# A two-convolution graph network on one core: the products of a finished tile are spread evenly over the visits of the next one

## The chip, the cores and the metric

The kernel runs on 1 core of one Trainium2 chip. The metric is the device time of one launch in microseconds (us), lower is better. The engines are named as in the profile: PE is TensorE's matmul stream and PEld its weight loads, DVE is VectorE, ACT is ScalarE, POOL is GpSimd, SP is SyncE. SPq and POOLq are the DMA issues of SP and POOL.

## The reference

There are 3,125 nodes of 1,024 features and 50,000 edges (`src` to `dst`, sorted by `dst`). A graph attention layer comes first, then the part that the change is in: two plain aggregates (mean over the neighbours), each followed by two products with 1,024 x 1,024 weights.

```python
def _sage_layer(h, edge_src, edge_dst, deg_inv, W_self, W_neigh, b):
    msg = h[edge_src]
    agg = jax.ops.segment_sum(msg, edge_dst, num_segments=h.shape[0])
    mean = agg * deg_inv[:, None]
    return h @ W_self + mean @ W_neigh + b
...
h = jax.nn.relu(_sage_layer(x, edge_src, edge_dst, deg_inv, W_self0, W_neigh0, b0))
out = _sage_layer(h, edge_src, edge_dst, deg_inv, W_self1, W_neigh1, b1)
...
h = jnp.maximum(_layernorm(x, axis=-1), 0.0)
x = x + _L1_gnn_ref(h, src, dst, L1_gnn_W_self0, L1_gnn_W_neigh0, L1_gnn_b0, L1_gnn_W_self1, L1_gnn_W_neigh1, L1_gnn_b1)
```

## The kernel before, in words

The program is a row of stages: tables of the edges, the attention layer's first product, its edge scores, its weighted sums (`weighted_sums`, gagg in the profile, a stage of gathers and short matmuls), `gat_finish`, then `first_layer` (agg0) and `last_layer` (agg1). Both of the last two have the same frame, and only they are changed.

**Numbers are kept in two halves.** A value is a pair of 16-bit floats, high and low, so a row is 2 x 1,024 values of 2 bytes (4 KB). A product with a weight that is also split takes three matmuls: high by high, high by low, low by high.

**Tiles and visits.** The nodes are cut into 25 tiles of 125 rows (`NT`, `TN`). The sum over the edges is made in 440 visits (`VISITS`), 17 or 18 for each tile. `place_of` lists them as pairs (i, n): tile i, and n, the number of the visit in the tile. A visit is:

- POOL gathers 128 rows of 4 KB by an indirect DMA into one of 7 buffers (`gather_visits`, L1885). It waits on `mm_done` of the visit 7 earlier.
- DVE makes the one-hot matrix `hot` 4 visits ahead (L1977, L2210).
- PE multiplies the gathered rows by it: `sum_window`, L1624, 16 matmuls of 64 columns into one of 3 PSUM buffers. It waits for `arrived` (the gather), `hot_ready`, and `added` of the visit 3 earlier.
- DVE adds the PSUM buffer to the sums in SBUF (L2016, L2240).

**A finished tile.** After the last visit of tile j, the sums of its rows are a factor of a product. ACT makes the high half (L2049, L2280), DVE the low half (`low`, L1983, L2216), and PE makes 48 products of 512 columns (`multiply`, L2095, L2318), in 12 pieces of 4. The pieces are put between the windows of the next tile, one in each of the visits n = `MULTIPLY_AT` to `MULTIPLY_AT` + 11. DVE reads the result out of PSUM (`read`, L1990, or the last operation of the last layer, L2250).

**The self part.** A tile's own rows are transposed by PE (`turn`, 16 transposes, L783), moved to SBUF by ACT (`move`, L2039, L2270) and multiplied by half of W_self1: 24 products of 512 columns (`multiply_self`, L2081, L2301). The first layer makes columns 0 to 511 of the last layer's self part and stores them (`part_rows`); the last layer makes columns 512 to 1,023. DVE reads them out (`read_part` L2001, `add_self` L2226). In the first layer the rows that are turned are the tile's output: DVE's `read`, ACT's relu and cast (L2056, L2061), DVE's `out_low` (L1994), `turn`.

**The order of the work** is written by hand. Each engine has its own loop over `place_of`, and the constants `LO_AT`, `MULTIPLY_AT`, `SELF_AT`, `TURN_AT` and so on say in which visit n a step is put, behind the window (PE) or the add (DVE) of that visit. Every engine works its list strictly in order, so a step that waits holds back the adds or windows behind it.

**SP's list in the last layer**, for each tile i: wait for `turned`, load the own rows of tile i + 1 (L2167); wait for `out_ready`, store the output of tile i - 1 (L2189); wait until it is stored; load x and the stored self part of tile i into the same buffers (`load_more`, L2172 and L2173). `add_self` waits for these loads, since its first operation adds them (L2223). Each transfer is two DMAs, of 112 and of 13 rows (`CUTS`).

Of the kernel before, what the change touches and what calls it, by code (L numbers as in the profile page):

```python
# [10 lines left out]
def bass_gat_sage_sage(nc, x_in, src_in, dst_in, w_gat, att_src, att_dst, gat_bias,  # L11
# [22 lines left out]
    NT = N // TN  # L34
# [112 lines left out]
    with top:  # L147
# [1742 lines left out]
        def first_layer(tag, flat, sums, mem):  # L1890

            with ExitStack() as ctx:
# [3 lines left out]
                AHEAD = 4  # L1896
                LO_AT, MULTIPLY_AT, READ_AT, OUT_AT = 0, 2, 14, 16
                PIECES = 12
                TURN_AT, SELF_AT, PART_AT = 1, 3, 15
                carve = carver(mem)  # L1900
# [67 lines left out]
                def _(v):  # L1968
# [57 lines left out]
                    v.wait_ge(added, VISITS)  # L2026
                    low(NT - 1)
                    read_part(NT - 2)
                    read(NT - 1)
# [4 lines left out]
                def _(a):  # L2034
# [9 lines left out]
                    for j in range(NT):  # L2044
                        tile = tile_reg_at(mybir.EngineType.Activation, j)
                        a.wait_ge(added, ended[j])
                        if j >= 1:
                            a.wait_ge(prod_done, j)
                        a.activation(as_turned(a_t, 0), by_feature(sums, tile), ACT.Copy, scale=sum_up[:, 0:1]).then_inc(hi_done, 1)  # L2049
                        if j >= 1:  # L2050
                            move(j - 1)
                        a.wait_ge(lo_done, j + 1)
                        a.activation(sums[:, ds(tile, 1), 0:D], ones[:, 0:1].to_broadcast([P, D]).rearrange("p (a d) -> p a d", a=1),
                                     ACT.Copy, scale=0.0).then_inc(zeroed, 1)
                        a.wait_ge(read_out, j + 1)
# [9 lines left out]
                def _(t):  # L2065
# [6 lines left out]
                    def multiply_self(j, piece):  # L2072
                        todo = half_products(half_ps, h_t, w_half)
                        per = len(todo) // PIECES
# [5 lines left out]
                        for o, l, r, start, stop in todo[piece * per:(piece + 1) * per]:  # L2080
                            last = t.matmul(o, l, r, start=start, stop=stop)  # L2081
                        if piece == PIECES - 1:
                            last.then_inc(self_done, 1)
# [15 lines left out]
                    for u, (i, n) in enumerate(place_of):  # L2099
# [12 lines left out]
                    for piece in range(PIECES):  # L2112
# [4 lines left out]
                    for piece in range(PIECES):  # L2117
                        multiply_self(NT - 1, piece)

        def last_layer(tag, flat, sums, mem):  # L2120

            with ExitStack() as ctx:
# [77 lines left out]
                def _(v):  # L2200
# [17 lines left out]

                    def add_self(j):
# [3 lines left out]
                        v.tensor_tensor(rows[:, :], rows[:, :], more[0:TN, :], ALU.add).then_inc(mixed, 1)  # L2223
                        v.wait_ge(mixed, j + 1)
                        v.wait_ge(self_done, j + 1)
# [7 lines left out]
                    for u, (i, n) in enumerate(place_of):  # L2233
# [8 lines left out]
                        if n == LO_AT and i >= 1:  # L2242
                            low(i - 1)
                        if n == ADD_AT and i >= 1:
                            add_self(i - 1)
# [5 lines left out]
                    v.wait_ge(added, VISITS)  # L2251
                    low(NT - 1)
                    add_self(NT - 1)
                    tile = tile_reg_at(mybir.EngineType.DVE, NT - 1)
                    v.wait_ge(self_read, NT)
# [29 lines left out]
                def _(t):  # L2285
# [6 lines left out]
                    def multiply_self(j, piece):  # L2292
                        todo = half_products(half_ps, h_t, w_half)
                        per = len(todo) // SELF_PIECES
# [5 lines left out]
                        for o, l, r, start, stop in todo[piece * per:(piece + 1) * per]:  # L2300
                            last = t.matmul(o, l, r, start=start, stop=stop)  # L2301
                        if piece == SELF_PIECES - 1:
                            last.then_inc(self_done, 1)
# [18 lines left out]
                    for u, (i, n) in enumerate(place_of):  # L2322
                        if n == 0:
                            turn(i)
# [63 lines left out]
```

## Time and profile before

| What | Value |
|---|---|
| Median of 3 runs | 3403.28 us (3386.56 to 3422.01) |
| Profiled execution: device time, span | 3406.57 us, 3404.8 us |
| PE busy | 2755.0 us (81%), 30361 matmuls |
| DVE busy | 2281.9 us (67%) |
| POOL busy | 1586.1 us (47%) |
| ACT busy | 1217.1 us (36%) |
| Moved by DMA | 923.25 MB, mean 271 GB/s |
| Granted TensorE clock | mean 0.911 |

The first layer lies between about 1610 and 2423 us of the span, the last layer from there to the end. Together they are more than half of the time. PEclk is the share of full speed that TensorE's clock had; it has two levels, 0.5 and 1.0. The DMA share is the mean busy time of the core's 16 DMA engines; over short stretches it can read a little above 1.

### The profile page before, as it was taken

The numbers are of one execution on the slowest core, as the hardware profiler recorded it, in microseconds if no ns is written. First come the engines' busy times: TensorE is split into PE (matmuls) and PEld (weight loads), VectorE is DVE, ScalarE is ACT, GpSimd is POOL, SyncE is SP. The second block draws the span as 40 slices with busy tenths as digits, with TensorE's granted clock in tenths as the row PEclk, the third lists the DMA queues.
The fourth block names the chain that finished last, engine by engine and source line by source line (L and its number), as shares of the span: only waits on it lengthen the run. The fifth ranks groups of instructions, "written<-read, shape, count | busy, mean of one in ns | idle before, by whom it ended". The sixth has DMA issues, their size and how long they took to land. (4 is left out here: it accounts for less than half of the span.)

```text
span 3404.8 us, 85744 instructions
## 1 busy us (share of the span) xinstructions
PE 2755.0 (81%) x30361; PEld 1840.4 (54%) x30361; DVE 2281.9 (67%) x4260; ACT 1217.1 (36%) x2842; POOL 1586.1 (47%) x1534
## 2 busy tenths in 40 slices
PE   5477898599999986997788888888567777777777
PEld 5244555388888863443555555555344444444444
DVE  7786778687888897885666666666245455555554
ACT  5464553698888863443122211221101000010010
POOL 2002232377777752222565655665244444454452
PEclk9878999799999998999798999999788888998888
DMA  2796995599999967775999988988588888898886
GB/s 77 244 294 211 323 325 175 170 340 348 354 348 352 349 213 242 224 217 187 355 317 303 317 303 307 311 305 277 212 257 270 258 269 246 264 286 256 262 284 190
DMA packets 282455, 923.25 MB, mean 271 GB/s; under 512 B 50690, under 2 KB 55790, under 8 KB 282030
## 3 DMA queue, kind: packets, MB, share of 16 engines
q0 software_dynamic: 209952, 697.51, 59.9%
q1 hardware_dynamic: 72078, 220.27, 21.0%
q8 instruction: 244, 4.00, 0.5%
q14 instruction: 181, 1.48, 0.1%
HBM read 857.98 MB, written 124.14 MB: 288 GB/s over the span
## 5 line engine op out<-in xcount | busy, mean ns | idle before, releaser
L1885 POOL DMA_INDIRECT agg_got<-h_rows,all_win_idx x756 | 780.2, 1032 | 775.3 <-PE agg_sum_ps L1624 583.2
L1614 PE MATMUL gagg_sum_ps<-gagg_got,gagg_hot_hi 128*128 128x256 f16 x3320 | 574.2, 273 | 63.9 <-DVE sums_acc L1560 27.1
L1624 PEld LDWEIGHTS agg_sum_ps<-all_mem,agg_got 128*128 128x128 f16 x12096 | 484.7, 103 | 240.1 <-issue 81.3
L1624 PE MATMUL agg_sum_ps<-all_mem,agg_got 128*128 128x64 f16 x12096 | 511.8, 200 | 80.8 <-DMA agg_got<-h_rows,all_win_idx 40.3
L1515 POOL DMA_INDIRECT gagg_got<-xs_rows,all_mem x415 | 465.0, 1120 | 167.8 <-issue 89.3
L1580 ACT ACTIVATE gagg_hot_hi<-gagg_hot,all_mem 128x128 f16<-128x128 f16 x1660 | 506.9, 387 | 84.1 <-DVE gagg_hot L1533 80.6
L2240 DVE TENSOR_TENSOR sums_acc<-agg_sum_ps,sums_acc 128x512 f32 x440 | 304.1, 691 | 287.7 <-PE agg_sum_ps L1624 283.2
L2016 DVE TENSOR_TENSOR sums_acc<-agg_sum_ps,sums_acc 128x512 f32 x440 | 303.7, 690 | 236.6 <-PE agg_sum_ps L1624 232.5
L1614 PE MATMUL gagg_sum_ps<-gagg_got,gagg_hot_lo 128*128 128x256 f16 x1660 | 453.7, 273 | 0.0
L2318 PE MATMUL agg_out_ps<-agg_w,all_mem 128*128 128x512 f16 x1152 | 341.6, 425 | 65.8 <-DVE all_mem L2216 65.8
L1614 PEld LDWEIGHTS gagg_sum_ps<-gagg_got,gagg_hot_hi 128*128 128x128 f16 x3320 | 285.7, 97 | 116.3 <-DVE sums_acc L1560 38.9
L2280 ACT ACTIVATE all_mem<-sums_acc,all_sum_up 128x1024 f16 x25 | 28.7, 1148 | 861.5 <-DVE sums_acc L2240 793.2
L2095 PE MATMUL agg_out_ps<-agg_w,all_mem 128*128 128x512 f16 x1200 | 318.9, 391 | 9.1 <-DVE all_mem L1983 8.8
L2301 PE MATMUL agg_half_ps<-agg_w_half,all_mem 128*128 128x512 f16 x600 | 179.7, 412 | 114.2 <-DVE all_mem L2226 110.4
L1538 DVE TENSOR_TENSOR gagg_hot_lo<-gagg_hot,all_mem 128x512 f16<-128x512 f16 x415 | 268.9, 687 | 4.0 <-DVE gagg_hot L1533 2.8
L1425 PE MATMUL edg_out_ps<-gatw_w,edg_a_t 128*128 128x512 f16 x1008 | 240.8, 383 | 17.7 <-ACT edg_rows L1233 17.6
L2056 ACT ACTIVATE all_mem<-all_mem,all_h_up 125x1024 f32<-125x1024 f32 x25 | 28.7, 1149 | 555.7 <-DVE all_mem L1990 555.7
L2318 PEld LDWEIGHTS agg_out_ps<-agg_w,all_mem 128*128 128x128 f16 x1152 | 101.7, 106 | 155.7 <-issue 102.1
L2081 PE MATMUL agg_half_ps<-agg_w_half,all_mem 128*128 128x512 f16 x600 | 179.4, 388 | 4.4 <-issue 4.4
L1885 POOL DMA_INDIRECT all_mem<-h_rows,all_win_idx x124 | 126.6, 1021 | 110.1 <-PE agg_sum_ps L1624 93.8
L1872 PE MATMUL fin_out_ps<-fin_w,all_mem 128*128 128x512 f16 x800 | 176.7, 379 | 0.0
L1614 PEld LDWEIGHTS gagg_sum_ps<-gagg_got,gagg_hot_lo 128*128 128x128 f16 x1660 | 162.2, 98 | 20.2
(404 smaller groups left out, 4084.9 us busy)
## 6 DMA issues: line engine op xcount, KB each, us to landing
gatw_piece<-slot_rows POOLq DMA_DIRECT2D x52, 512.0 KB
split_w<-edg_w_out SPq DMA_DIRECT2D x32, 512.0 KB, 8.8
x_rows<-fin_val POOLq DMA_DIRECT2D x25, 500.0 KB
h_rows<-fin_h POOLq DMA_DIRECT2D x25, 500.0 KB, 8.2
agg_got<-h_rows,all_win_idx POOLq DMA_INDIRECT x756
norm_x_sb<-in_x_dram SPq DMA_DIRECT2D x25, 448.0 KB
fin_x_sb<-in_x_dram SPq DMA_DIRECT2D x25, 448.0 KB
all_mem<-xp_rows SPq DMA_DIRECT2D x25, 448.0 KB
```

Source lines behind the costliest of these rows:

```text
L1425: last = t.matmul(o, l, r, start=start, stop=stop)
L1515: g.indirect_dma_start(out=got[:, u % R, :], out_offset=None, in_=rows_in[:, :], in_offset=bass.IndirectOffsetOnAxis(ap=set_idx[:, col:col ...
L1538: v.tensor_tensor(hot_lo[:, u % HOTS, :, :], hot[:, u % HOTS:u % HOTS + 1, :].to_broadcast([P, H, P]), weight_e[:, ds(begins[g] + j, 1), 1 ...
L1580: last = a.activation(hot_hi[:, u % HOTS, h, :], hot[:, u % HOTS, :], ACT.Copy, scale=high_e[:, ds(begins[g] + j, 1), h])
L1614: last = t.matmul(sum_ps[g % 2][:, h * C:(h + 1) * C], hot_k[:, u % HOTS, h, :], got[:, u % R, part * D + h * C:part * D + (h + 1) * C], s ...
L1624: last = t.matmul(sum_ps[:, k * WIN:(k + 1) * WIN], got_u[:, part * D + k * P:part * D + (k + 1) * P], hot_u, start=(part == 0), stop=(par ...
L1885: g.indirect_dma_start(out=got[u % slots], out_offset=None, in_=rows_in[:, :], in_offset=bass.IndirectOffsetOnAxis(ap=win_idx[:, u:u + 1], ...
L2016: v.tensor_tensor(window_of(flat, at), sum_ps[u % SUMS][:, :].rearrange("p (k d) -> p k d", k=KT), window_of(flat, at), ALU.add).then_inc( ...
L2095: last = t.matmul(o, l, r, start=start, stop=stop)
L2240: v.tensor_tensor(window_of(flat, at), sum_ps[u % SUMS][:, :].rearrange("p (k d) -> p k d", k=KT), window_of(flat, at), ALU.add).then_inc( ...
L2301: last = t.matmul(o, l, r, start=start, stop=stop)
L2318: last = t.matmul(o, l, r, start=start, stop=stop)
```

## The change

The constants of both layers are set anew, and three steps move in the text of the program.

- **PE.** In the first layer, the 48 products move from n = 2 to 13 to n = 3 to 14; the self part's 24 products, before 2 in each of n = 3 to 14 beside the 4 of the other product, go to five visits of their own: 5, 5, 5, 5 and 4 at n = 15, 16, 0, 1, 2. `turn` goes from n = 1 to n = 3. In the last layer the products move in the same way from n = 2 to 13 to n = 3 to 14, the self part from 3 in each of n = 7 to 14 to the same five visits, and `turn` from n = 0 to n = 13.
- **DVE.** `low` goes from n = 0 to 1 in both. In the first layer `read` goes from 14 to 15, `out_low` from 16 to 0 of the tile after, `read_part` from 15 to 4 of the tile after. In the last layer `add_self` is cut in two: `mix` (the add of what was loaded) at n = 12 and the read-out of the self part at n = 13, where both stood at n = 5; the last operation of a tile goes from 14 to 15.
- **ACT.** In the first layer, `move` comes behind the clearing of the sums and no more ahead of it.

Nothing is added and nothing taken away: the number of matmuls, of DVE and ACT operations and of DMAs is the same.

```diff
-                LO_AT, MULTIPLY_AT, READ_AT, OUT_AT = 0, 2, 14, 16
+                OUT_AT, LO_AT, MULTIPLY_AT, READ_AT = 0, 1, 3, 15
                 PIECES = 12
-                TURN_AT, SELF_AT, PART_AT = 1, 3, 15
+                TURN_AT, PART_AT = 3, 4
+                SELF_AT = (15, 16, 0, 1, 2)
...
+                        if n == OUT_AT and i >= 2:
+                            out_low(i - 2)
                         if n == LO_AT and i >= 1:
                             low(i - 1)
+                        if n == PART_AT and i >= 3:
+                            read_part(i - 3)
                         if n == READ_AT and i >= 1:
                             read(i - 1)
-                        if n == PART_AT and i >= 2:
-                            read_part(i - 2)
-                        if n == OUT_AT and i >= 1:
-                            out_low(i - 1)
...
-                        if SELF_AT <= n < SELF_AT + PIECES and i >= 2:
-                            multiply_self(i - 2, n - SELF_AT)
+                        if n in SELF_AT:
+                            piece = SELF_AT.index(n)
+                            j = i - 2 if piece < 2 else i - 3
+                            if j >= 0:
+                                multiply_self(j, piece)
...
-                LO_AT, MULTIPLY_AT, ADD_AT, DONE_AT = 0, 2, 5, 14
+                LO_AT, MULTIPLY_AT, MIX_AT, ADD_AT, TURN_AT, DONE_AT = 1, 3, 12, 13, 13, 15
                 PIECES = 12
-                SELF_AT, SELF_PIECES = 7, 8
+                SELF_AT = (15, 16, 0, 1, 2)
...
-                        if SELF_AT <= n < SELF_AT + SELF_PIECES:
-                            multiply_self(i, n - SELF_AT)
+                        if n in SELF_AT:
+                            piece = SELF_AT.index(n)
+                            j = i if piece < 2 else i - 1
+                            if j >= 0:
+                                multiply_self(j, piece)
+                    for piece in range(2, len(SELF_AT)):
+                        multiply_self(NT - 1, piece)
```

PE in the last layer, at the turn from one tile to the next, before. agg_sum_ps is written by the windows, agg_half_ps by the self products, agg_turn_ps by `turn`, agg_out_ps by the 48 products.

```order
L2301 MATMUL agg_half_ps<-agg_w_half,all_mem 128x512 x3
L1624 MATMUL agg_sum_ps<-all_mem,agg_got 128x64 x48
L783 MATMUL agg_turn_ps<-all_ident,all_mem 128x128 x16
L1624 MATMUL agg_sum_ps<-all_mem,agg_got 128x64 x16
L1624 MATMUL agg_sum_ps<-all_mem 128x64 x16
L1624 MATMUL agg_sum_ps<-all_mem,agg_got 128x64 x16
L2318 MATMUL agg_out_ps<-agg_w,all_mem 128x512 x4
```

The same place after the change (L2314 is the self product, L2331 the other):

```order
L2314 MATMUL agg_half_ps<-agg_w_half,all_mem 128x512 x5
L1624 MATMUL agg_sum_ps<-all_mem,agg_got 128x64 x16
L2314 MATMUL agg_half_ps<-agg_w_half,all_mem 128x512 x5
L1624 MATMUL agg_sum_ps<-all_mem,agg_got 128x64 x16
L2314 MATMUL agg_half_ps<-agg_w_half,all_mem 128x512 x4
L1624 MATMUL agg_sum_ps<-all_mem,agg_got 128x64 x16
L2331 MATMUL agg_out_ps<-agg_w,all_mem 128x512 x4
```

Six windows in a row with only `turn` between them have become windows with 4 or 5 products behind each.

DVE in the last layer, where the loaded rows and the self part are taken in, before (n = 5). The ISA and TENSOR_LOAD rows read a register; L2223 is the add of what SP loaded, L2226 reads the self part.

```order
L2240 ISA
L2240 TENSOR_TENSOR sums_acc<-agg_sum_ps,sums_acc 128x8x64
L2223 TENSOR_TENSOR all_mem<-all_mem 125x1024
L2226 SCALAR_TENSOR_TENSOR all_mem<-agg_half_ps,agg_post_self,all_mem 125x512
L196 TENSOR_LOAD all_win_at
```

After (n = 12 and n = 13; L2231 is the add, L2236 the read-out):

```order
L2250 TENSOR_TENSOR sums_acc<-agg_sum_ps,sums_acc 128x8x64
L2231 TENSOR_TENSOR all_mem<-all_mem 125x1024
L196 TENSOR_LOAD all_win_at
L196 ISA x2
L2218 TENSOR_SCALAR all_mem<-all_iota_tn,all_win_rel 128x64
L2250 ISA
L2250 TENSOR_TENSOR sums_acc<-agg_sum_ps,sums_acc 128x8x64
L2236 SCALAR_TENSOR_TENSOR all_mem<-agg_half_ps,agg_post_self,all_mem 125x512
```

The pair has moved seven visits towards the end of the tile, and a visit's work now stands between its two operations.

## Rows read from the trace of the kernel before

**Rows 1.** Busy time by stretch: gather stage gagg, first layer, last layer
```profile
core 0: us, PE busy (x) PEld busy (x) DVE busy (x) ACT busy (x) POOL busy (x), PEclk, DMA share, GB/s
700.00:1100.00 400.00, 387.26 (x3928) 339.25 (x3926) 323.78 (x633) 345.98 (x1193) 315.00 (x280) 1.00 0.96 351
1736.87:2382.66 645.79, 559.79 (x7753) 367.96 (x7751) 418.69 (x820) 128.33 (x106) 382.36 (x363) 0.93 0.89 306
2516.66:3384.26 867.60, 663.45 (x8456) 408.08 (x8456) 460.90 (x898) 67.01 (x47) 402.01 (x398) 0.88 0.86 263
```

**Rows 2.** ACT's high half, once a tile, 22 of the first layer: start, duration, [idle before]
```profile
1736.87 1.15 ACT L2049 ACTIVATE all_mem<-sums_acc,all_sum_up 128x1024 f16 x1 [2.14 <-DVE sums_acc L2016]
...
2382.66 1.15 ACT L2049 ACTIVATE all_mem<-sums_acc,all_sum_up 128x1024 f16 x1 [1.98 <-DVE sums_acc L2016]
```

**Rows 3.** The same, 24 of the last layer, first and last
```profile
2516.66 1.15 ACT L2280 ACTIVATE all_mem<-sums_acc,all_sum_up 128x1024 f16 x1 [28.27 <-DVE sums_acc L2240]
...
3384.26 1.15 ACT L2280 ACTIVATE all_mem<-sums_acc,all_sum_up 128x1024 f16 x1 [32.58 <-DVE sums_acc L2240]
```

**Rows 4.** Who waited for whom, 1737 to 2383 us: total, times, longest
```profile
PE agg_turn_ps L783 <- DVE all_mem L1994: 60.7, 21, 4.0
```

**Rows 5.** Who waited for whom, 2517 to 3384 us
```profile
DVE all_mem L2223 <- DMA all_mem<-part_rows: 124.0, 23, 10.1
...
PE agg_half_ps L2301 <- DVE all_mem L2226: 110.4, 23, 9.6
...
PE agg_out_ps L2318 <- DVE all_mem L2216: 65.0, 23, 3.7
```

**Rows 6.** Timeline of PE at full clock: windows, and turn
```profile
2060.14 0.63 PE L1624 MATMUL agg_sum_ps<-all_mem,agg_got 128*128 128x64 f16 x16
2060.60 1.03 PE L2095 MATMUL agg_out_ps<-agg_w,all_mem 128*128 128x512 f16 x4
...
2061.90 0.63 PE L1624 MATMUL agg_sum_ps<-all_mem,agg_got 128*128 128x64 f16 x16
...
2899.96 0.63 PE L1624 MATMUL agg_sum_ps<-all_mem,agg_got 128*128 128x64 f16 x16
2900.43 1.06 PE L783 MATMUL agg_turn_ps<-all_ident,all_mem 128*128 128x128 f16 x16
2901.70 0.63 PE L1624 MATMUL agg_sum_ps<-all_mem,agg_got 128*128 128x64 f16 x16 [0.21 <-DVE sums_acc L2240]
```

**Rows 7.** Timeline of POOL, gathers with free buffers
```profile
2071.66 0.99 POOL L1885 DMA_INDIRECT agg_got<-h_rows,all_win_idx  x1 [0.30 <-PE agg_sum_ps L1624]
2072.96 0.99 POOL L1885 DMA_INDIRECT agg_got<-h_rows,all_win_idx  x1 [0.30 <-issue]
```

**Rows 8.** Timeline of one tile's output, store and loads, last layer
```profile
2899.51 1.28 DVE L2250 SCALAR_TENSOR_TENSOR all_mem<-agg_out_ps,agg_post,all_mem 125x1024 f32<-125x1024 f32 x1
...
2906.90 0.35 SPq L2172 DMA_DIRECT2D all_mem<-x_rows  x1
...
2920.22 1.22 DVE L2223 TENSOR_TENSOR all_mem<-all_mem 125x1024 f32<-125x1024 f32 x1 [6.43 <-DMA all_mem<-part_rows]
```

**Rows 9.** Timeline from a tile's last add to its first product
```profile
2903.51 0.69 DVE L2240 TENSOR_TENSOR sums_acc<-agg_sum_ps,sums_acc 128x512 f32 x1
...
2904.33 1.15 ACT L2280 ACTIVATE all_mem<-sums_acc,all_sum_up 128x1024 f16 x1 [36.88 <-DVE sums_acc L2240]
...
2907.17 1.02 PE L2318 MATMUL agg_out_ps<-agg_w,all_mem 128*128 128x512 f16 x4 [2.19 <-DVE all_mem L2216]
```

**Rows 10.** Busy time in stretches of 2 us (columns as in Rows 1)
```profile
2056.00:2058.00 2.00, 2.00 (x25) 1.17 (x24) 1.15 (x3) 0.00 (x0) 0.99 (x1) 1.00 1.03 419
...
2904.00:2906.00 2.00, 0.63 (x16) 0.54 (x16) 1.48 (x4) 1.67 (x2) 1.39 (x3) 1.00 0.92 271
2906.00:2908.00 2.00, 0.83 (x4) 0.42 (x5) 1.96 (x5) 1.25 (x1) 1.78 (x1) 1.00 0.93 322
2908.00:2910.00 2.00, 2.00 (x21) 1.14 (x20) 1.73 (x4) 0.00 (x0) 1.30 (x2) 0.58 0.89 287
```

More of the change, by code:

```diff
@@ L2017, in _ @@
                                         ALU.add).then_inc(added, 1)
+                        if n == OUT_AT and i >= 2:
+                            out_low(i - 2)
                         if n == LO_AT and i >= 1:
                             low(i - 1)
+                        if n == PART_AT and i >= 3:
+                            read_part(i - 3)
                         if n == READ_AT and i >= 1:
                             read(i - 1)
-                        if n == PART_AT and i >= 2:
-                            read_part(i - 2)
-                        if n == OUT_AT and i >= 1:
-                            out_low(i - 1)
                     v.wait_ge(added, VISITS)
+                    out_low(NT - 2)
                     low(NT - 1)
+                    read_part(NT - 3)
                     read_part(NT - 2)
@@ L2049, in _ @@
                         a.activation(as_turned(a_t, 0), by_feature(sums, tile), ACT.Copy, scale=sum_up[:, 0:1]).then_inc(hi_done, 1)
-                        if j >= 1:
-                            move(j - 1)
                         a.wait_ge(lo_done, j + 1)
@@ L2054, in _ @@
                                      ACT.Copy, scale=0.0).then_inc(zeroed, 1)
+                        if j >= 1:
+                            move(j - 1)
                         a.wait_ge(read_out, j + 1)
@@ L2073, in multiply_self @@
                         todo = half_products(half_ps, h_t, w_half)
-                        per = len(todo) // PIECES
+                        last_piece = len(SELF_AT) - 1
                         if piece == 0:
@@ L2079, in multiply_self @@
                                 t.wait_ge(part_ready, j)
-                        for o, l, r, start, stop in todo[piece * per:(piece + 1) * per]:
+                        for o, l, r, start, stop in todo[5 * piece:5 * (piece + 1)]:
                             last = t.matmul(o, l, r, start=start, stop=stop)
-                        if piece == PIECES - 1:
+                        if piece == last_piece:
                             last.then_inc(self_done, 1)
@@ L2108, in _ @@
                             multiply(i - 1, n - MULTIPLY_AT)
-                        if SELF_AT <= n < SELF_AT + PIECES and i >= 2:
-                            multiply_self(i - 2, n - SELF_AT)
+                        if n in SELF_AT:
[4 more added lines that the diff above has]
+                    for piece in range(2, len(SELF_AT)):
+                        multiply_self(NT - 3, piece)
                     turn(NT - 2)
-                    for piece in range(PIECES):
+                    for piece in range(len(SELF_AT)):
                         multiply_self(NT - 2, piece)
@@ L2116, in _ @@
                     turn(NT - 1)
-                    for piece in range(PIECES):
+                    for piece in range(len(SELF_AT)):
                         multiply_self(NT - 1, piece)
@@ L2217, in low, with mix @@
                                                ALU.mult, ALU.subtract).then_inc(lo_done, 1)
-                    def add_self(j):
+                    def mix(j):
                         v.wait_ge(x1_loaded, CUT * (j + 1))
@@ L2223, in add_self @@
                         v.tensor_tensor(rows[:, :], rows[:, :], more[0:TN, :], ALU.add).then_inc(mixed, 1)
+                    def add_self(j):
                         v.wait_ge(mixed, j + 1)
@@ L2243, in _ @@
                             low(i - 1)
+                        if n == MIX_AT and i >= 1:
+                            mix(i - 1)
                         if n == ADD_AT and i >= 1:
@@ L2252, in _ @@
                     low(NT - 1)
+                    mix(NT - 1)
                     add_self(NT - 1)
@@ L2293, in multiply_self @@
                         todo = half_products(half_ps, h_t, w_half)
-                        per = len(todo) // SELF_PIECES
+                        last_piece = len(SELF_AT) - 1
                         if piece == 0:
@@ L2299, in multiply_self @@
                                 t.wait_ge(self_read, j)
-                        for o, l, r, start, stop in todo[piece * per:(piece + 1) * per]:
+                        for o, l, r, start, stop in todo[5 * piece:5 * (piece + 1)]:
                             last = t.matmul(o, l, r, start=start, stop=stop)
-                        if piece == SELF_PIECES - 1:
+                        if piece == last_piece:
                             last.then_inc(self_done, 1)
@@ L2322, in _ @@
                     for u, (i, n) in enumerate(place_of):
-                        if n == 0:
+                        if n == TURN_AT:
                             turn(i)
@@ L2331, in _ @@
                             multiply(i - 1, n - MULTIPLY_AT)
-                        if SELF_AT <= n < SELF_AT + SELF_PIECES:
-                            multiply_self(i, n - SELF_AT)
+                        if n in SELF_AT:
[3 more added lines that the diff above has]
+                                multiply_self(j, piece)
+                    for piece in range(2, len(SELF_AT)):
+                        multiply_self(NT - 1, piece)
                     ready(NT - 1)
```

## The prediction

> **What bounds the kernel now.** I read the profile's page first: PE is busy 81% of the span, more than any other, so it looks like the bound. The busy time by stretch corrects this [rows 1]. In the gather stage before the two layers PE is busy 387.26 of 400 us at clock 1.00, and the DMA engines, at share 0.96, move 351 GB/s. In the first layer PE is busy 87%, the DMA share is 0.89 and the rate 306 GB/s; in the last layer 76%, 0.86 and 263. Neither engine is full in either layer: they take turns.
>
> Next, the time of one tile, from the operation that ACT makes once a tile. First layer: (2382.66 - 1736.87) / 21 = 30.75 us [rows 2]. Last layer: (3384.26 - 2516.66) / 23 = 37.72 us [rows 3].
>
> Then the waits. In the first layer PE stands before `turn` 21 times, 60.7 us in all, so 2.9 us a tile, for DVE's `out_low` (L1994) [rows 4]. In the last layer DVE waits 124.0 us for the loads of x and the stored self part, 23 times, 5.4 us each; PE waits 110.4 us for the read-out behind that add, 4.8 us a tile, and 65.0 us, 2.8 a tile, for the low half [rows 5]. The 5.4 and the 4.8 are one stall seen from two engines.
>
> Last, the pace of single visits. A first-layer visit with window, 4 products and 2 self products takes 2061.90 - 2060.14 = 1.76 us, of which the window is 2060.60 - 2060.14 = 0.46, so a product is 1.30 / 6 = 0.217 us; `turn` costs PE 2901.70 - 2900.43 = 1.27 us [rows 6]. A visit with no product behind it is as fast as POOL issues gathers, 2072.96 - 2071.66 = 1.30 us [rows 7].
>
> **The floors of a tile.** 440 / 25 = 17.6 visits, 72 products, one `turn`.
>
> - PE at full clock: 17.6 x 0.46 + 72 x 0.217 + 1.27 = 8.1 + 15.6 + 1.3 = 25.0 us.
> - POOL: 17.6 x 1.30 = 22.9 us. DVE: 418.69 / 21 = 19.9 and 460.90 / 23 = 20.0 us [rows 1].
> - Bytes: 306 GB/s x 30.75 us = 9.41 MB, and 263 x 37.72 = 9.92 MB.
>
> So before, twelve visits of a first-layer tile are PE's (21.1 us, in which the gathers run only as fast as buffers come free) and the rest are POOL's and the waits'. If the same 72 products are 4 or 5 in each visit, a visit costs PE 0.46 + 4 x 0.217 = 1.33 or 0.46 + 5 x 0.217 = 1.55 us, near what POOL needs, and what binds next is the transfers. The bound of their time comes from two sides:
>
> - Below: the rate of the gather stage, 351 GB/s. 9.41 / 0.351 = 26.8 us and 9.92 / 0.351 = 28.3 us. That stage has no loads and stores of SP in between.
> - Above: packets go on taking as long as in the layer itself. 306 / 0.89 x 0.96 = 330 GB/s gives 28.5 us; 263 / 0.86 x 0.96 = 294 GB/s gives 33.8 us.
>
> I take 27.6 us for the first layer, the middle: its rate in short stretches reaches 419 GB/s [rows 10]. For the last I take 31.7 us, above its middle of 31.1, since SP's transfers are more there and each visit can now wait for its gather.
>
> **The waits, step by step.** A shorter tile needs each wait gone and none new.
>
> - First layer, `turn`. `out_low` is at n = 0 and `turn` at n = 3; `read` at n = 15 starts relu and cast on ACT, about 2.3 us, beside two visits. PE then has n = 0, 1, 2, 1.55 + 1.55 + 1.33 = 4.4 us, against DVE's 1.2. The 2.9 us go.
> - Low half, both layers. Last add to first product is 2907.17 - 2903.51 = 3.66 us [rows 9]. `low` and the first product keep their distance of two visits, but the windows ahead of it now carry products: from the end of the last window PE has 4.4 + 0.46 = 4.9 us of work (6.2 with `turn`). `low` stands behind the adds of n = 0 and 1, the second of which can begin at 2.0 us, so it ends near 4.2. The 2.8 us go, with 0.7 us to spare; if they did not, they would cost at most 2.8 again.
> - Last layer, loads. The chain is the last operation of a tile (L2250), store, wait for it, loads, add: 2920.22 - 2899.51 = 20.7 us to the add's start, of which 13.3 are from the first load's issue [rows 8]. It had from n = 14 to n = 5, 8.6 visits; it gets n = 15 to n = 12, 14.6 visits, 14.6 x 31.7 / 17.6 = 26.3 us. `load_row`, released by `turn` at n = 13 instead of n = 0, now goes into SP's queue ahead of the store: 0.5 MB, some 2 us. Spare: 3.6 us. The 5.4 us go. If the loads are late, DVE stands at n = 12 with its adds behind it, and PE stops within three windows, since there are three PSUM buffers.
> - Last layer, own rows. `turn` at n = 13, then ACT's move of some 2 us, against PE's 0.46 + 0.87 + 1.33 + 0.46 = 3.1 us to the first self product at n = 15: hidden.
> - ACT's `move` behind the clearing of the sums: ACT is busy 128.33 of 645.79 us; hidden by 12 visits.
>
> **The sum**, against the profiled execution's 3406.6 us (the three runs have the median 3403.3, 0.1% off). First layer: 22 tiles with all their products x (30.75 - 27.6 = 3.15) = 69 us. Last layer: 23 x (37.72 - 31.7 = 6.0) = 138 us. The start of the last layer is full of transfers of weights and stays, but its self products no more wait for their weights and the second tile has the stall too: 10 us. At the ends of both layers 14 self products come behind the last window, 3 us each, where PE waits for the low half anyway: 0. 3406.6 - 69 - 138 - 10 = 3190 us (3189.6).
>
> **Rivals.**
>
> 1. The transfers reach the gather stage's rate. 22 x 3.95 + 23 x 9.4 + 10 = 313 us: 3093. For it: the share there is 0.96 with PE just as busy. Against: SP's transfers. The Trainium skill (DMA: Bandwidth & Descriptors, Specifications) gives a limit of about 358 GB/s from HBM for one core. By that figure tiles would take 26.3 and 27.7 us, an estimate that makes the sum 3069. The stage's 351 agrees, the 419 GB/s of one stretch [rows 10] is above it.
> 2. Packets keep today's mean time, 28.5 and 33.8 us. 22 x 2.25 + 23 x 3.9 = 140 us: 3267.
> 3. The change does half of what it says: SP's chain is drawn out, since the DMA engines are now full all through the tile, and the last layer's stall only moves to n = 12. Then only the first layer gains: 3406.6 - 69 = 3338. It needs a chain of over 14.6 / 17.6 x 37.7 = 31 us instead of 20.7.
> 4. Slower: the clock. PE falls to the 0.5 level after 2 us stretches in which it was busy 0.63 and 0.83 us [rows 10]; each tile now has such drops, mean 0.93 and 0.88 [rows 1]. If PE, short of gathers, idles a little in every visit, the drops could come all through the tile. At a mean of 0.68 its 25.0 us become 36.8: 22 x (36.8 - 30.75) - 23 x (37.72 - 36.8) = 133 - 21 = +112 us, 3518. It begins to be slower where the mean falls under 25.0 / 34.3 = 0.73. Against: a PE that is slowed is busy again, and in the gather stage it stayed at 1.00 for 400 us. The Trainium skill (TensorE: Matmul & The Clock Gate, "A second HAM failure mode: psum-queue depth-cycling") tells of a kernel whose short idle times between groups of matmuls made the clock go up and down. By that rule this rival is the case; the trace shows drops only behind stretches with long idle time.
>
> **How the numbers follow.** Forecast 3190: 0.50. Rival 1: 0.16. Rival 2: 0.19. Rival 3: 0.08. Rival 4: 0.04. The rest, 0.03, is within 1%. A measurement of this kernel tells about 1% from no change, 34 us, so faster is under 3369: 0.50 + 0.16 + 0.19 + 0.08 = 0.93. I give 0.91, and 0.05 to same, for what I have not seen in the waits. The range goes from rival 1 to a little above rival 2: 3090 to 3290.
>
> **What would show it.** Right: the once-a-tile operation of ACT comes every 27 to 28 and 31 to 32 us; DMA share 0.94 or more and 320 to 345 GB/s in both layers; PE's waits for L1994, L2216 and L2226 near zero; its waits are now for gathers, and short. Wrong: DVE waits 2 us or more a tile at the add at n = 12 (rival 3); PEclk under 0.85 (rival 4); a share near 0.96 at 300 GB/s or less (rival 2).

## The result, and the profile after

The changed kernel takes 3112.18 us (median of 4 runs, 3109.58 to 3119.44), the one before 3398.49 us in the same runs: ratio 0.9153, 95% interval 0.9100 to 0.9207. The forecast was 3190 us in a range of 3090 to 3290. The direction came out as forecast, and the waits that the forecast named went; the size is 1.3 times as large, 286 us in place of 217.

The busy time by stretch of the changed kernel: the gather stage, then the first and the last layer (columns as in [rows 1], which these answer to).

```profile
700.00:1100.00 400.00, 390.45 (x3968) 342.67 (x3965) 328.04 (x638) 349.84 (x1207) 314.39 (x282) 1.00 0.97 354
1724.77:2295.96 571.19, 529.27 (x7756) 332.31 (x7755) 416.24 (x819) 127.58 (x106) 382.47 (x364) 1.00 0.96 346
2417.41:3090.16 672.75, 587.14 (x8492) 362.30 (x8491) 457.55 (x898) 69.58 (x46) 421.85 (x399) 1.00 1.01 341
```

The gather stage has not moved. The two layers do the same work in less time: the DMA share went from 0.89 to 0.96 and from 0.86 to 1.01, the clock from 0.93 and 0.88 to 1.00. The stretches run from one high half of ACT to another, so they give the time of a tile: 571.19 / 21 = 27.20 us (before 30.75 [rows 2]) and 672.75 / 23 = 29.25 us (before 37.72 [rows 3]).

Who waited for whom in the first layer of the changed kernel, against [rows 4]:

```profile
POOL agg_got L1885 <- issue: 86.5, 211, 3.2
PEld agg_sum_ps L1624 <- DMA agg_got<-h_rows,all_win_idx: 73.0, 93, 2.5
...
PE agg_sum_ps L1624 <- DMA agg_got<-h_rows,all_win_idx: 35.9, 50, 2.0
```

And in the last layer, against [rows 5]:

```profile
PE agg_sum_ps L1624 <- DMA agg_got<-h_rows,all_win_idx: 76.0, 82, 2.6
...
DVE all_mem L2231 <- DMA all_mem<-part_rows: 1.2, 1, 1.2
PE agg_out_ps L2331 <- DVE all_mem L2224: 0.7, 1, 0.7
```

All four waits that the prediction named are gone: 60.7 us before `turn` to nothing, 124.0 to 1.2, 110.4 to nothing, 65.0 to 0.7. What PE now waits for are gathers, many times and briefly.

The profile's chain of work that ended last, in shares of the span, names the same thing. Before, its largest piece was `all_mem<-part_rows`, the loads behind the stall:

```profile
DMA all_mem<-part_rows 6%; PE agg_out_ps L2318 4%; DMA out_dram<-all_mem 4%; PE agg_half_ps L2301 4%; PE agg_sum_ps L1624 3%; SPq L2172 1%; DVE all_mem L2250 1%; DVE all_mem L2223 1%; DMA all_mem<-h_rows 1%; DVE all_mem L2226 1%; SPq L788 0%; SPq L2173 0%; PE agg_out_ps L2338 0%; SPq L2189 0%; DVE sums_acc L2240 0%
```

After, it is the gathers:

```profile
DMA 14%; issue 5%; POOL 3%; PE 3%; DVE 0%; ACT 0%; POOLq 0%; DVEq 0%; ACTq 0%
DMA agg_got<-h_rows,all_win_idx 11%; POOL agg_got L1885 3%; DMA all_mem<-h_rows,all_win_idx 2%; PE agg_sum_ps L1624 1%; PE agg_half_ps L2314 1%; PE agg_out_ps L2331 0%; POOL all_mem L1885 0%; PE agg_out_ps L2356 0%; PE agg_turn_ps L783 0%; DVE all_mem L2224 0%; ACT all_mem L2293 0%; DVE all_mem L2209 0%; DVE agg_got L2239 0%; POOLq L1884 0%; DVE all_mem L2275 0%
```

Twelve kernels follow. Their tiles are measured in the same way, here from the second high half of each layer to the last. Each ratio is against runs of the kernel before on the same chip, whose median was 3389.76 to 3404.7 us. Each tile comes from one profiled execution. Kernels with the very same layer differ there by up to 0.3 us in the changed first layer (26.8 to 27.1), 0.2 in the changed last one (29.2 to 29.4) and 0.7 in the last one of before (37.0 and 37.7), so smaller differences show nothing. In short:

| Run | Time (us) | Ratio, 95% interval | Tile of first, last layer (us) |
|---|---|---|---|
| before | 3398.49 | 1 | 30.8, 37.7 |
| changed | 3112.18 | 0.9153 (0.9100 to 0.9207) | 27.1, 29.3 |
| e1 first layer only | 3307.08 | 0.9718 (0.9672 to 0.9765) | 26.9, 37.0 |
| e2 last layer only | 3199.95 | 0.9407 (0.9375 to 0.9439) | 30.9, 29.2 |
| e3 loads' add at n = 5 | 3263.76 | 0.9602 (0.9570 to 0.9634) | 26.9, 35.8 |
| e4 uneven, stall gone | 3278.14 | 0.9648 (0.9615 to 0.9681) | 30.5, 32.3 |
| e5 half the gathers, changed | 2950.09 | 0.8686 (0.8645 to 0.8726) | 24.8, 25.4 |
| e6 half the gathers, before | 3248.91 | 0.9565 (0.9518 to 0.9612) | 30.7, 32.3 |
| e7 1 of 24 self products | 3096.51 | 0.9117 (0.9064 to 0.9169) | 26.8, 29.6 |
| e8 before, PE kept busy | 3378.73 | 0.9953 (0.9924 to 0.9983) | 30.1, 37.6 |
| e9 uneven, DVE spread | 3200.78 | 0.9403 (0.9372 to 0.9433) | 30.7, 29.3 |
| e10 own rows behind loads | 3152.68 | 0.9267 (0.9241 to 0.9293) | 26.8, 31.1 |
| e11 `turn` at n = 1 | 3122.75 | 0.9174 (0.9149 to 0.9200) | 27.3, 29.4 |
| e12 own rows later | 3149.42 | 0.9276 (0.9246 to 0.9306) | 26.8, 31.2 |

### The profile page after: what moved, and what is told of

It reads as the page before. It is cut to its first block and busy times, and to the rows that moved or that the text cites. A ratio compares the mean times of both kernels' runs of the same rounds, so it can differ in the third digit from the quotient of the medians.

```text
span 3107.8 us, 85745 instructions
## 1 busy us (share of the span) xinstructions
PE 2645.8 (85%) x30361; PEld 1756.8 (57%) x30361; DVE 2278.2 (73%) x4260; ACT 1219.4 (39%) x2842; POOL 1598.8 (51%) x1534
## 5 line engine op out<-in xcount | busy, mean ns | idle before, releaser
L1885 POOL DMA_INDIRECT agg_got<-h_rows,all_win_idx x756 | 788.8, 1043 | 513.0 <-PE agg_sum_ps L1624 217.0
L1624 PEld LDWEIGHTS agg_sum_ps<-all_mem,agg_got 128*128 128x128 f16 x12096 | 447.6, 100 | 379.9 <-DMA agg_got<-h_rows,all_win_idx 277.1
L1624 PE MATMUL agg_sum_ps<-all_mem,agg_got 128*128 128x64 f16 x12096 | 489.4, 196 | 177.1 <-DMA agg_got<-h_rows,all_win_idx 176.3
L1614 PEld LDWEIGHTS gagg_sum_ps<-gagg_got,gagg_hot_hi 128*128 128x128 f16 x3320 | 286.1, 97 | 111.2 <-DVE sums_acc L1560 37.6
L2098 PE MATMUL agg_out_ps<-agg_w,all_mem 128*128 128x512 f16 x1200 | 309.0, 382 | 0.0
L2331 PE MATMUL agg_out_ps<-agg_w,all_mem 128*128 128x512 f16 x1152 | 297.9, 381 | 0.7 <-DVE all_mem L2224 0.7
L2283 ACT ACTIVATE all_mem<-agg_turn_ps 128x2048 f16<-128x2048 f16 x25 | 46.9, 1877 | 545.8 <-PE agg_turn_ps L783 545.8
L1533 DVE TENSOR_SCALAR gagg_hot<-all_iota_tn,all_mem 128x128 f16<-128x128 f32 x415 | 112.1, 292 | 85.5 <-PE gagg_sum_ps L1614 84.8
L1560 DVE TENSOR_TENSOR sums_acc<-gagg_sum_ps,sums_acc 125x1033 f32 x135 | 165.7, 1228 | 5.3 <-PE gagg_sum_ps L1614 2.3
L1885 POOL DMA_INDIRECT all_mem<-h_rows,all_win_idx x124 | 135.1, 1090 | 65.7 <-issue 36.9
L1425 PEld LDWEIGHTS edg_out_ps<-gatw_w,edg_a_t 128*128 128x128 f16 x1008 | 93.2, 99 | 114.6 <-issue 25.2
```

The source lines that it names most:

```text
L1614: last = t.matmul(sum_ps[g % 2][:, h * C:(h + 1) * C], hot_k[:, u % HOTS, h, :], got[:, u % R, part * D + h * C:part * D + (h + 1) * C], s ...
L1624: last = t.matmul(sum_ps[:, k * WIN:(k + 1) * WIN], got_u[:, part * D + k * P:part * D + (k + 1) * P], hot_u, start=(part == 0), stop=(par ...
L1885: g.indirect_dma_start(out=got[u % slots], out_offset=None, in_=rows_in[:, :], in_offset=bass.IndirectOffsetOnAxis(ap=win_idx[:, u:u + 1], ...
```

## The experiments

**Each layer alone (e1, e2).** The edit is the change, in one of the two functions only.

> The change in the first layer alone; the last layer is the one of before. The traces give the first layer's share as 84 us (24 tiles, 30.6 to 27.1 us each), so about 3315 us if the two layers' gains simply add. If the first layer's gain needs the last layer's (or a slower one follows from it), the two single runs don't add up to 286 us.

> The change in the last layer alone. By the traces 195 us in 23 tiles (37.7 to 29.25 us) and 17 us at its start and end: about 3188 us, tile 29.3 us.

Measured: 3307.08 us and 3199.95 us. The ratios take off 2.8% and 5.9%, together 8.7%, and the whole change 8.5%: the two gains add within their intervals. Two thirds are the last layer's.

**The stall back, the products even (e3).** In the last layer:

```diff
-                LO_AT, MULTIPLY_AT, MIX_AT, ADD_AT, TURN_AT, DONE_AT = 1, 3, 12, 13, 13, 15
+                LO_AT, MULTIPLY_AT, MIX_AT, ADD_AT, TURN_AT, DONE_AT = 1, 3, 5, 13, 13, 15
```

> The changed kernel, but in the last layer the add of the loaded rows stands at n = 5 again, with all else spread as it is. If the old stall was SP's chain of store, wait and loads (20.7 us, against 7.6 visits x 1.66 = 12.6 us), it comes back with 6 to 8 us: tile about 35 to 36 us, 3250 to 3270 us, DVE waits 100 us or more for the loads. If an even spread alone made the difference, the loads land in time and the kernel stays at 3112 us.

Measured: 3263.76 us, 35.8 us a tile. The waits of its last layer:

```profile
DVE all_mem L2231 <- DMA all_mem<-part_rows: 223.4, 23, 11.7
PEld agg_sum_ps L1624 <- issue: 203.7, 88, 10.3
PE agg_sum_ps L1624 <- DVE sums_acc L2250: 174.6, 23, 9.8
```

The loads are late by 9.7 us each time, and since DVE's adds queue behind the waiting one, PE stops three windows later for 7.6 us. So the stall was SP's chain of store, wait and loads, and what took it away is the place of one add, 7 visits later: 6.5 us a tile against the changed kernel. The stall is longer here than before (5.4 us [rows 5]). Two reasons lie in the lists, not tested apart: the last operation of a tile, which releases the store, stands at n = 15 and not 14, and the load of the own rows now goes ahead of the store.

**The stall gone, the products uneven (e4).** The later read-outs stay; the self products go back beside the others, one tile later:

```diff
-                SELF_AT = (15, 16, 0, 1, 2)
+                SELF_AT = tuple(range(3, 15))
...
-                        for o, l, r, start, stop in todo[5 * piece:5 * (piece + 1)]:
+                        for o, l, r, start, stop in todo[2 * piece:2 * (piece + 1)]:
```

(with `PART_AT` = 15 in the first layer, `ADD_AT` = 15 and `TURN_AT` = 1 in the last).

> The changed kernel with its later read-outs and loads, but the self part's 24 products again 2 in each of n = 3 to 14 beside the 4 of the other product (6 products in 12 visits, none in the others), one tile later, in both layers. Theory that the transfers set the pace and 7 buffers smooth the rest: first layer 28.5 us, last 30 us a tile, about 3160 us. Rival, that light visits cost what they did (POOL's pace there and the clock's drops behind them): first layer back at 30.7, last 31 or more, about 3230 us. Rival, that only the waits mattered: 3112 us.

Measured: 3278.14 us, worse than all three expected. The busy time of its two layers, and one wait of each:

```profile
1727.30:2372.98 645.68, 571.34 (x7748) 373.82 (x7746) 416.02 (x820) 129.79 (x107) 373.06 (x363) 0.93 0.89 306
2508.72:3250.85 742.13, 633.77 (x8470) 394.39 (x8471) 456.66 (x898) 69.59 (x47) 426.11 (x398) 0.92 0.95 308
...
PE agg_turn_ps L783 <- DVE all_mem L1995: 31.5, 21, 2.1
...
PE agg_out_ps L2331 <- DVE all_mem L2224: 56.5, 23, 3.6
```

The first of these lines is that of the kernel before, digit for digit in the clock, the share and the rate. So the first of the two rivals, that the light visits (those without products) cost what they did, is right for the first layer: without the even order nothing is gained there. The wait before `turn` is not gone here but halved, 1.5 us a tile in place of 2.9; e9 below takes it away wholly. My own theory, that 7 buffers smooth the rest, fell. In the last layer both count. With e3 they make a rough square: 37.7 us with neither, 35.8 with the even order only, 32.3 with only the stall gone, 29.25 with both. It is rough because e3's stall is longer than that of before, and because in e4 PE still waits 2.5 us a tile for the low half (2.8 before): that wait goes with the even order (1.2 us in all 23 tiles of e3).

**What in the uneven visits costs the time (e8, e9).** First the clock. e8 is the kernel before, with work of no use ahead of the windows where PE was idle:

```diff
+                        if i >= 1 and (n >= 15 or n <= 1):
+                            for _ in range(4):
+                                t.matmul(sum_ps[u % SUMS][:, :], w_half[:, 0, 0, 0:P], w_half[:, 0, 0, :], start=True, stop=True)
```

(from tile 3 on in the first layer).

> The kernel before with 4 products of no use put ahead of the windows of n = 15, 16, 17, 0 and 1 in both layers: more work for PE, in the visits where it was near idle and its clock fell behind them. If the clock's drops cost time by themselves, the first layer falls by 1 to 2 us a tile and the last by 1 to 3, in spite of more work: about 3320 us, PEclk over 0.95. If only the waits cost time, it stays at 3400 us or goes above.

Measured: 3378.73 us. The first layer:

```profile
1730.10:2360.77 630.67, 605.74 (x8137) 378.02 (x8135) 418.07 (x820) 128.23 (x105) 369.47 (x363) 1.00 0.90 313
```

The clock is at 1.00, and a tile takes 30.1 us, 0.7 less, with more work in it: 384 matmuls more in 21 tiles, at 0.217 us 4.0 us a tile. In the last layer the mean clock rose only to 0.92, with DVE still waiting for the loads 23 times, and the tile stayed within 0.1 us. The 0.7 us are a net figure, since the added work may cost time too: the drops cost at least that. They can't have cost more than about 2.2 us of the 30.75 (an estimate: all that a mean clock of 0.93 withholds, (1 - 0.93) x 30.75, as if every moment of it held up the tile). So of the first layer's 3.6 us, 1.4 or more have another cause than the clock. The whole kernel gained 0.5%, much less than the 3320 us expected.

Second, DVE. e9 has e4's first layer, with DVE's `out_low` and `read_part` taken out of the light visits' neighbourhood:

```diff
-                OUT_AT, LO_AT, MULTIPLY_AT, READ_AT = 0, 1, 3, 15
+                OUT_AT, LO_AT, MULTIPLY_AT, READ_AT = 4, 1, 3, 15
...
-                TURN_AT, PART_AT = 3, 15
+                TURN_AT, PART_AT = 7, 2
```

> The changed kernel with the uneven first layer of the fourth run (6 products in each of n = 3 to 14), but DVE's out_low at n = 4, turn at n = 7 and read_part at n = 2: two of DVE's per-tile operations leave the light visits' neighbourhood n = 15 to 0, and turn (1.3 us of PE) goes among the dense ones. The last layer is the changed one. In the fourth run the first layer took 30.7 us a tile, and in the light visits PE waited for DVE's adds. If DVE's crowding there sets them (5.6 light visits x 0.88 + 1.28 + 1.23 + 0.75 + 1.28 = 9.5 us, with 21.1 us of dense visits 30.6), the tile falls by about 1 us, to 29.7. If unevenness as such costs the 3.6 us (POOL's pace in the light visits and the clock), it stays at 30.7: 3112 + 24 x 3.6 = about 3200 us.

Measured: 3200.78 us, 30.7 us a tile: no gain. Its largest waits of PE in the first layer:

```profile
PE agg_out_ps L2099 <- DVE all_mem L1984: 39.6, 21, 2.6
PE agg_sum_ps L1624 <- DVE sums_acc L2017: 36.3, 36, 1.9
```

No wait before `turn` is left, so that wait by itself was worth nothing. The wait has another name each time, L1994 before, DVE's adds and `turn` in e4, the low half and the adds here, and the tile is 30.5 to 30.8 us in all three. Twelve visits at 1.76 us, 21.1 us, are PE's in all of them, so about 9.6 us go to the five or six light visits. What may bind there is the chain of the last add, ACT's high half, DVE's low half and the first product, 3.66 us [rows 9], which bare windows of 0.46 us don't cover; that is argued, not tested. POOL's pace of 1.30 us a visit, the other half of the rival, is not what PE waits for: its waits for `agg_got` are 4.3 us in all 640 us here. That one order's wait comes back as another's is shown; why the sum is so nearly the same in all three is not.

**Are the transfers the bound now? (e5, e6, e7)** Half of the gathers' bytes are left out (rows with a number of 1562 or more are not fetched), which leaves all other work as it is:

```diff
-            last_row = g.to_reg(N - 1)
+            last_row = g.to_reg(N // 2 - 1)
```

> The changed kernel, but rows with a number of 1562 or more are not gathered in the two layers (half of the gathers' bytes left out, same number of gathers and all the matmuls). If the transfers set the time, the tiles fall to PE's 25.0 us (27.1 and 29.25 now): 24 x 2.1 + 23 x 4.25 = about 150 us less, 2960 us, PE busy over 97%. If PE or the order sets it, it stays at 3112 us.

> The kernel before with the same half of the gathers' bytes left out. Theory: its first layer is set by PE in the dense visits, POOL in the light ones and the wait before turn, not by bytes: 30 to 30.7 us a tile. Its last layer waits for SP's chain, which runs faster through emptier DMA engines: 31 to 34 us. About 3250 to 3320 us in all. If bytes set both layers before as well, it falls as far as the changed kernel does, to 3250 us or less with the first layer under 28 us.

> The changed kernel with 1 of the 24 self products in each tile (23 left out, 5.0 us of PE work a tile). Transfer theory: the last layer's tile stays within 1 us of 29.25 and the first layer falls from 27.1 to 25 to 26 us (9.41 MB at 370 to 385 GB/s): about 3050 us. Rival, PE sets the pace: 5.0 us less in each of 47 tiles, about 2880 us.

The changed kernel with half the gathers:

```profile
1713.96:2234.98 521.02, 518.86 (x7756) 338.40 (x7755) 416.32 (x819) 127.46 (x107) 381.94 (x364) 1.00 0.74 217
2348.66:2932.15 583.49, 572.28 (x8492) 370.65 (x8491) 456.68 (x898) 69.59 (x47) 420.05 (x399) 1.00 0.83 233
```

PE is busy 99.6% and 98.1%, and a tile takes 24.8 and 25.4 us, where PE's own 25.0 us had been worked out. The kernel before with the same half:

```profile
1727.20:2371.80 644.60, 559.28 (x7756) 367.76 (x7754) 418.56 (x820) 128.26 (x105) 381.49 (x363) 0.93 0.62 175
2490.50:3232.34 741.84, 624.62 (x8456) 392.41 (x8456) 460.67 (x898) 67.00 (x46) 416.20 (x399) 0.93 0.68 183
```

Its first layer does not move, with the DMA engines busy 62%: the bytes left out were not on the path. Its last layer gains 5.5 us a tile; there the wait for the loads fell from 124.0 to 46.8 us, so the chain of the loads got shorter. The total alone, 3248.91 us, would have fitted the rival too (3250 us or less); the first layer decides, and it was to be under 28 us for that. And with 23 of the 24 self products left out of the changed kernel:

```profile
1723.05:2288.11 565.06, 465.26 (x7254) 310.86 (x7254) 413.93 (x819) 127.43 (x107) 378.07 (x363) 0.94 0.97 350
2402.99:3083.81 680.82, 528.10 (x7960) 348.55 (x7960) 456.89 (x898) 69.58 (x46) 418.01 (x399) 0.89 1.00 337
```

5.0 us of PE work less a tile give nothing beyond the spread of single executions in the first layer (26.8 us; other kernels with the changed first layer have 26.8 to 27.1) and nothing in the last. POOL has the same number of gathers to issue in e5, whose tiles are shorter, so it is not the bound either. So the transfers set the pace of both layers now, in the first even more so than I had expected (25 to 26 us; 9.41 MB at the rates named with it even make 24.4 to 25.4).

**Where SP's transfers stand (e10, e12).** The rate at which full DMA engines move bytes was the number that I had wrong. In the kernel before, SP sends its loads in one go from 2906.90 on [rows 8]: x, the stored self part and the own rows, 1.25 MB. In the changed one the own rows go apart. e10 puts them together again:

```diff
-                        if i + 1 < NT:
-                            sp.wait_ge(turned, i + 1)
-                            load_row(i + 1)
                         if i >= 1:
...
                             load_more(i)
+                        if i + 1 < NT:
+                            sp.wait_ge(turned, i + 1)
+                            load_row(i + 1)
```

> The changed kernel, but in the last layer SP issues the load of a tile's own rows right behind the loads of x and the stored self part, so 1.25 MB come in one row as in the kernel before, instead of 0.75 and 0.5 MB apart. Theory that bunched loads of SP beside full gather buffers lower the rate (before, 306 GB/s at full share; after, 338): the last layer's tile rises from 29.25 to 30.5 to 32 us, 3140 to 3175 us. Rival, that the rate depends on the mix of bytes alone: 3112 us.

Measured: 3152.68 us, 31.1 us a tile, the same bytes. Its last layer:

```profile
2418.09:3132.82 714.73, 596.45 (x8492) 373.21 (x8491) 456.32 (x898) 69.60 (x47) 426.79 (x399) 0.98 0.98 321
```

Stretches of 3 us of it, from SP's loads on (the first is issued at 2826.8, the own rows at 2831.6):

```profile
2826.00:2829.00 3.00, 3.00 (x42) 1.86 (x43) 2.54 (x7) 0.00 (x0) 2.29 (x3) 1.00 1.01 376
2829.00:2832.00 3.00, 3.00 (x43) 1.90 (x42) 2.17 (x5) 0.00 (x0) 2.23 (x3) 1.00 1.03 326
2832.00:2835.00 3.00, 1.83 (x29) 0.98 (x28) 1.40 (x4) 0.00 (x0) 1.98 (x2) 1.00 1.02 281
2835.00:2838.00 3.00, 1.49 (x26) 0.77 (x23) 0.91 (x2) 0.00 (x0) 0.99 (x1) 1.00 1.05 270
2838.00:2841.00 3.00, 1.31 (x20) 0.58 (x16) 0.92 (x2) 0.00 (x0) 0.99 (x1) 1.00 1.04 287
2841.00:2844.00 3.00, 2.85 (x41) 1.66 (x42) 1.50 (x3) 0.00 (x0) 0.99 (x1) 1.00 1.03 366
```

The engines are full in all six, and for 9 us they move 270 to 287 GB/s, against 366 and 376 at the two ends, while PE is busy half the time for want of gathers. In the changed kernel the dip behind the loads is shorter, and a second one comes where the own rows (issued at 2823.9) and the store (2828.5) now stand; PE is busy all through that one:

```profile
2809.00:2812.00 3.00, 3.00 (x47) 1.87 (x43) 1.91 (x5) 0.00 (x0) 2.32 (x3) 1.00 1.05 360
2812.00:2815.00 3.00, 2.58 (x40) 1.54 (x39) 1.75 (x4) 0.00 (x0) 2.23 (x3) 1.00 1.02 289
2815.00:2818.00 3.00, 1.51 (x23) 0.78 (x20) 0.91 (x2) 0.00 (x0) 0.99 (x1) 1.00 1.05 293
2818.00:2821.00 3.00, 2.69 (x42) 1.50 (x39) 1.57 (x3) 0.00 (x0) 1.33 (x2) 1.00 1.02 371
...
2824.00:2827.00 3.00, 3.00 (x45) 1.84 (x43) 2.51 (x6) 0.84 (x1) 2.09 (x3) 1.00 0.94 298
2827.00:2830.00 3.00, 3.00 (x43) 1.88 (x42) 2.96 (x6) 0.81 (x1) 1.90 (x3) 1.00 1.02 259
```

The slower rate is not all of e10's 1.8 us. Divided by the share, its last layer moves 321 / 0.98 = 328 GB/s at full share, the changed one 341 / 1.01 = 338: 3% for the rate, and another 3% for engines that are less full. With the latter goes a wait for the low half that is back:

```profile
PE agg_out_ps L2331 <- DVE all_mem L2224: 17.5, 21, 1.4
```

e12 was to make use of that. It is e10 with one more wait ahead of the own rows:

```diff
+                            sp.wait_ge(mm_done, ended[i] + 7)
```

> A try at a faster version: the changed kernel, but SP issues the load of a tile's own rows when the 8th visit or so of the tile has begun (it waits for mm_done), between the loads of x and the store, instead of right ahead of the store. Theory that SP's transfers cost less the further apart they come (the run before, with 1.25 MB in one row, rose to 31.1 us a tile, 319 GB/s): the tile falls from 29.25 to 28.5 to 29.0 us, 3095 to 3108 us. Rival, that the gap is wide enough already or that a late load of the rows makes turn wait at n = 13: 3112 us or more.

Measured: 3149.42 us, 37 us above the changed kernel. SP's issues in it show why:

```profile
2819.53 0.35 SPq L2180 DMA_DIRECT2D all_mem<-x_rows  x1
...
2824.21 0.87 SPq L2175 DMA_DIRECT2D all_mem<-h_rows  x2
```

Store and wait take so long that the loads of x start only 4.7 us ahead of the visit that I had picked, and the own rows are in the same bunch as in e10. The try tells nothing about a real gap. No run that does all the work was faster than the changed kernel.

**Only the wait before `turn` back (e11).** In the first layer:

```diff
-                OUT_AT, LO_AT, MULTIPLY_AT, READ_AT = 0, 1, 3, 15
+                OUT_AT, LO_AT, MULTIPLY_AT, READ_AT = 16, 1, 3, 15
...
-                TURN_AT, PART_AT = 3, 4
+                TURN_AT, PART_AT = 1, 4
```

(`out_low` again for the tile whose `read` was the visit before.)

> The changed kernel, but in the first layer out_low and turn are where they were (n = 16 of the same tile, n = 1), with the even products. PE waits 1 to 2 us a tile before turn again, by the lists. If the transfers set the tile's time there too, that wait is covered (PE's 25.0 + 1.5 is under 27.1): 27.1 to 27.5 us, 3112 to 3120 us. If each wait of PE is paid in full, the tile is 28.6 us or more: 3150 us.

Measured: 3122.75 us, 27.3 us a tile. PE waits for L1995 again:

```profile
PE agg_turn_ps L783 <- DVE all_mem L1995: 27.9, 20, 2.0
```

That is 1.4 us a tile, half of the 2.9 before, and the tile is 0.2 to 0.5 us above those of the other kernels with the changed first layer. The whole kernel is 10.6 us slower by the medians, 0.4 us for each of 24 tiles, but the two ratios' intervals overlap. So the wait is mostly covered. Gathers land during it: PE's own waits for `agg_got` fell from 35.9 us to 10.0.

## Why the prediction was right, and where its size was off

- **What bounds it before: right that no engine is full, wrong that PE and the DMA engines take turns in the first layer.** If they did, half the bytes would have shortened it; in e6 the tile stayed at 30.7 us. PE waited there for DVE and, in the kernel before, for practically no gather (0.2 us in 646). The prediction's other account of the same tile, twelve visits of PE's and the rest POOL's and the waits', is nearer, but without POOL, since a PE that followed POOL's pace would be waiting for gathers.
- **The waits: right that all go, wrong about one price.** The walk through the four chains held: three of them left nothing, the loads 1.2 us in 23 tiles. But the 2.9 us before `turn` were named among the causes of the first layer's time. e9 and e11 show that they have no such price: with them gone and the products uneven nothing is gained, with half of them back and the products even 0.2 to 0.5 us are lost. No term of the sum rested on it, since the tile was worked out from the transfers.
- **The floors: right.** 25.0 us for PE, measured as 24.8 and 25.4 in e5.
- **First layer, 22 x 3.15 = 69 us: 22 x 3.55 = 78 measured** (27.2 us in place of 27.6).
- **Last layer, 23 x 6.0 = 138 us: 23 x 8.47 = 195 measured.** This is the term that was mis-sized. The step was the choice of 31.7 us, "above its middle", between 28.3 and 33.8. The upper end took two things from the layer as it was: a share of 0.96 at most, which became 1.01, and packets as slow as then, 306 GB/s at full share, which became 341 / 1.01 = 338. The slowness belonged in part to the order being changed: e10, with SP's loads together again, takes 1.8 us a tile more for unchanged bytes and has 328 GB/s at full share. That is 10 of the 32 GB/s between 306 and 338; where the other 22 come from is not shown. The right end to lean to was the gather stage's 351, that is rival 1, whose sum of 3093 is nearer to the measured 3112 than mine. That the total still lay in the range is because the range reached down to that rival.
- **Start and end, 10 us: 17 measured** (from the first to the second high half of the last layer 48.2 us before, 34.4 after, and 3 at the end). The three terms make 290 of the 297 us between the two profiled executions (3406.57 and 3109.58 us); most of the rest is in the first layer's first tiles, which were put at nothing (84 us from its first high half to its last). The medians differ by 286.
- **Rivals 2 and 3 did not come.** For rival 3, SP's chain had to be longer than 31 us; the loads were late once in 23 tiles.
- **Rival 4, the clock, came out on the other side.** The clock went to 1.00, not down. The rule of the Trainium skill on short idle times (TensorE: Matmul & The Clock Gate, "A second HAM failure mode: psum-queue depth-cycling") is not what happens here: PE is busy 87% in the changed last layer, with 82 short waits for gathers, and keeps 1.00. The first layer before had PE busy 87% too, but with 21 waits of 2.9 us before `turn`, up to 4.0, and 0.93. The drops return in e7, where PE is busy 78% and its waits for gathers are up to 5.1 us long: 0.89.
- The limit that the Trainium skill gives (DMA: Bandwidth & Descriptors, Specifications), about 358 GB/s, which it works out by dividing the stack's rate by two cores, lies a little above the means of whole layers, 341 to 346. It is no limit for short stretches of this kernel, which runs on one core: 376 in e10, 419 before [rows 10].

## What to carry to other kernels

When no engine is full, add up each one's work per period first: the gain of an even order is the distance to the largest of the sums, and single waits in the trace are not to be added up, since one can be covered (1.4 us of PE for 0.2 to 0.5 us here) or come back under another name. Where the next bound is the transfers, don't size it with the rate of the stretch that is being reordered; take the rate of a neighbouring stage that keeps the engines full. In an engine that works its list in order, the place of one operation that waits for a long chain can be worth more than all the work that is spread (in the last layer 6.5 us a tile from e3, 3.0 from e4).

## What was not expected of the hardware

- The DMA engines at full share move between 254 GB/s (the kernel before, 2912 to 2914 us, share 1.00; the changed one has 259 at 2827) and 419 GB/s [rows 10]. The low values shown come when SP's loads or its store run beside the gathers; the same 9.9 MB a tile took 29.25 or 31.1 us by the place of one 0.5 MB load alone. Whether it is the bunch or the neighbour in the queue (the store in one, the loads in the other) was not told apart.
- To lift the granted clock from 0.93 to 1.00 gave 0.7 us of a 30.8 us tile net of the added work (e8), out of at most about 2.2 by the estimate above. At least in part the lower clock comes where PE waits for others anyway. In one tile of the kernel before, `turn` takes 1.89 us in place of the 1.06 of [rows 6], right behind a wait of 2.06 us:

```profile
2044.76 1.89 PE L783 MATMUL agg_turn_ps<-all_ident,all_mem 128*128 128x128 f16 x16 [2.06 <-DVE all_mem L1994]
```
